# Four blocks in one transfer, or two and two: splitting an early load of a conditional residual kernel

## The reference

```python
# L0: a weight per sample, folded from 8 masked weights
w_bot = einsum('bg,got->bot', y, weight * mask)
x = x + einsum('bnt,bot->bno', x, w_bot) + bias
# L1: base linear layer and 8 LoRA pairs of rank 16, weighted by cond_8, scaled by 2
h = einsum('btc,erc->bter', x, As)
x = x + x @ W_base.T + b_base + 2 * einsum('bter,eor,be->bto', h, Bs, w)
# L2: top 2 of 8 experts (gelu(gate) * up, hidden 512) and one shared expert of the same form
# L3: one expert of 8 by argmax (silu(up) * gate, hidden 256, with biases)
```

## Time and profile before

| what | value |
|---|---|
| median of 3 runs | 137.72 us (137.63 to 138.63) |
| profiled execution | 138.17 us |
| its span, first to last instruction | 136.3 us |
| TensorE busy | 131.7 us |
| VectorE, ScalarE, GpSimd busy | 102.0, 99.4, 75.4 us |
| granted TensorE clock | 1.00 throughout |

### The profile page before, as it was taken

How to read it: one execution, slowest core, us unless ns; L and a number is a source line. 1 busy time by engine, 2 the same in 40 slices (tenths; PEclk the granted TensorE clock), 3 DMA queues, 4 the chain that set the end, 5 groups by cost and what they waited for, 6 DMA issues and landing times.

```text
span 136.3 us, 3164 instructions
## 1 busy us (share of the span) xinstructions
PE 131.7 (97%) x866; PEld 119.4 (88%) x866; DVE 102.0 (75%) x201; ACT 99.4 (73%) x205; POOL 75.4 (55%) x89
## 2 busy tenths in 40 slices
PE   7899999999999999999999999999999999999990
PEld 5778888888888879999999999999999999999990
DVE  0599898797757666668877687767878677887892
ACT  3774797979964659777797777756757669889870
POOL 0148369776991045468496684963452635325770
PEclk9999999999999999999999999999999999999999
DMA  4999999997002974674764657646577474755134
GB/s 141 356 404 407 408 400 402 396 402 301 7 0 93 373 302 190 279 281 197 300 267 197 257 224 293 282 184 267 225 282 297 172 287 195 290 239 227 45 112 154
DMA packets 11489, 34.54 MB, mean 253 GB/s; under 512 B 1104, under 2 KB 2512, under 8 KB 11472
## 3 DMA queue, kind: packets, MB, share of 16 engines
q1 hardware_dynamic: 11184, 34.15, 63.8%
q10 hardware_dynamic: 288, 0.20, 0.5%
HBM read 12.32 MB, written 1.05 MB: 98 GB/s over the span
## 4 chain that ended last, share of the span: by engine, by line
PE 75%; DMA 7%; POOL 7%; DVE 3%; SPq 3%; issue 2%; ACT 2%; DVEq 0%; POOLq 0%; ACTq 0%
PE up L297 26%; PE gate L297 26%; PE acc L297 23%; POOL slabs L765 7%; DMA w_gu<-slabs 4%; DMA slabs<-third_in 3%; SPq L223 1%; DVE up L930 1%; SPq L280 1%; ACT slabs L640 1%; DVE x_res L910 1%; DVE x_res L939 1%; ACT h_pair L635 0%; DVE x_lo L902 0%; ACT x_hi L612 0%
## 5 line engine op out<-in xcount | busy, mean ns | idle before, releaser
L772 POOL TENSOR_TENSOR dn_lo<-slabs,dn_hi 128x256 fp32r<-128x256 f32 x40 | 29.6, 741 | 40.5 <-ACT dn_hi L653 40.5
L629 ACT ACTIVATE h_act<-gate 128x512 f32<-128x512 f32 x48 | 28.8, 601 | 26.2 <-PE gate L297 24.9
L922 DVE TENSOR_TENSOR h_pair<-up,h_pair 128x512 fp32r<-128x512 f32 x55 | 37.6, 683 | 0.0
L932 DVE SCALAR_TENSOR_TENSOR up<-h_act,w_route,up 128x512 f32<-128x512 f32 x32 | 24.2, 756 | 17.0 <-PE up L297 16.6
L297 PE MATMUL gate<-x_hi,w_gu 128*128 128x256 f32 x160 | 35.2, 282 | 0.2 <-DMA w_gu<-slabs 0.2
L297 PE MATMUL up<-x_hi,w_gu 128*128 128x256 f32 x158 | 34.5, 281 | 0.0
L635 ACT ACTIVATE h_pair<-up 128x512 fp32r<-128x512 f32 x55 | 32.8, 597 | 0.0
L297 PEld LDWEIGHTS gate<-x_hi,w_gu 128*128 128x128 f32 x160 | 27.3, 188 | 1.0 <-issue 0.9
L297 PE MATMUL acc<-h_pair,dn_hi 128*128 128x512 f32 (+1 forms) x76 | 27.5, 377 | 0.0
L297 PEld LDWEIGHTS up<-x_hi,w_gu 128*128 128x128 f32 x158 | 27.0, 188 | 0.0
L297 PE MATMUL gate<-x_lo,w_gu 128*128 128x256 f32 x80 | 22.4, 280 | 0.0
(11 more groups left out here) (128 smaller groups left out, 203.0 us busy)
## 6 DMA issues: line engine op xcount, KB each, us to landing
w_gu<-slabs SPq DMA_DIRECT2D x40, 512.0 KB, 3.0
slabs<-slabs_moe SPq DMA_DIRECT2D x8, 768.0 KB, 13.5
slabs<-slabs_l SPq DMA_DIRECT2D x4, 768.0 KB, 8.7
sh_raw<-slabs_shared SPq DMA_DIRECT2D x2, 384.0 KB, 5.3
x_res<-x_rest SPq DMA_DIRECT2D x1, 768.0 KB, 7.0
outT<-x_res SPq DMA_DIRECT2D x6, 128.0 KB, 1.9
slabs<-second_in SPq DMA_DIRECT2D x1, 320.0 KB, 3.1
slabs<-third_in SPq DMA_DIRECT2D x1, 256.0 KB, 4.2
```

Source lines behind the costliest of these rows:

```text
L629: nc.scalar.activation(h_act[:, u % 2, :], gate_ps[u % 2][:], ACT.Gelu_apprx_tanh).then_inc(act_done, 1)
L772: nc.gpsimd.tensor_tensor(dn_lo[:, q % W_SLOTS, :], slab_cols(at, DOWN_AT, 256), dn_hi[:, q % W_SLOTS, :].bitcast(F32), ALU.subtract).then ...
L922: V.tensor_tensor(h_lo[:, u % H_SLOTS, :], h_of(u), h_hi[:, u % H_SLOTS, :].bitcast(F32), ALU.subtract).then_inc(h_lo_done, 1)
L932: ins = V.scalar_tensor_tensor(h_of(u), h_act[:, k, :], weight, h_of(u), ALU.mult, ALU.mult)
```

## The change

third_in is cut in two. Blocks 6 and 7 stay in it, 128 KB. The mask and the LoRA down matrix become a transfer mask_in of their own, 128 KB too, with a semaphore d_mask. It is issued on SP right behind the third, ahead of the fourth. DVE waits for d_mask where it waited for d_third; TensorE still waits for d_third before block 6, and has a new wait for d_mask before lora(0,2). Addresses in the on-chip memory stay as they were, since the two buffers lie side by side.

```diff
-        third_sb = early(4, P)
+        third_sb = early(2, P)
+        mask_sb = early(2, P)
-        lora_bT, mask, lora_a = second_sb[:, 4, :], third_sb[:, 2, :], third_sb[:, 3, :]
+        lora_bT, mask, lora_a = second_sb[:, 4, :], mask_sb[:, 0, :], mask_sb[:, 1, :]
...
             sp.dma_start(third_sb[:, :, :], third_in).then_inc(d_third, DMA)
+            sp.dma_start(mask_sb[:, :, :], mask_in).then_inc(d_mask, DMA)
             sp.dma_start(fourth_sb[:, :, :], fourth_in).then_inc(d_fourth, DMA)
...
+            pe.wait_ge(d_mask, DMA)
             pe.wait_ge(bw_ready, 1)
             lora(gate_ps[0][:, 0:S], 0, 2)
...
-            dve.wait_ge(d_third, DMA)
+            dve.wait_ge(d_mask, DMA)
...
-    third = cat([w_l0[:, 6:], a(L0_cond_mask)[:, None], as_[:, None]], axis=1)
+    mask_in = np.stack([a(L0_cond_mask), as_], axis=1)
...
-        "second_in": second, "third_in": third, "fourth_in": fourth,
+        "second_in": second, "third_in": w_l0[:, 6:], "mask_in": mask_in, "fourth_in": fourth,
```

More of the change, by code:

```diff
@@ L67, with build @@
 C_COLS = C_W + 2 * P
-def build(nc, x_first, first_in, second_in, third_in, fourth_in, x_rest, slabs_moe, slabs_l3, slabs_shared, outT):
+def build(nc, x_first, first_in, second_in, third_in, mask_in, fourth_in, x_rest, slabs_moe, slabs_l3, slabs_shared, outT):
     with ExitStack() as ctx:
@@ L169, in build @@
         m_banks = [None, gate_ps[1][:, 0:S], up_ps[1][:, 0:S], acc_ps[:, S:2 * S]]
-        d_first, d_second, d_third, d_fourth, d_x, d_x_rest = (
-            sem(n) for n in ("d_first", "d_second", "d_third", "d_fourth", "d_x", "d_x_rest"))
+        d_first, d_second, d_third, d_mask, d_fourth, d_x, d_x_rest = (
+            sem(n) for n in ("d_first", "d_second", "d_third", "d_mask", "d_fourth", "d_x", "d_x_rest"))
         d_expert = [sem(f"d_expert{e}") for e in range(E)]
```

## The result

| what | before | after |
|---|---|---|
| median of 22 runs each | 137.90 us | 138.54 us |
| ratio after / before | | 1.0048, 95% interval 1.0027 to 1.0069 |
| profiled execution, its span | 138.17, 136.3 us | 138.54, 136.7 us |

The ratio and its interval rest on the fast runs alone; of the changed kernel's 22, three stand outside (139.64, 140.68, and 218.46 us at a granted clock of 0.567), and the median of the other 19 is 138.45.

What follows compares the result with a forecast made beforehand. The front bounds the kernel: from the third transfer through mask and DVE to TensorE's almost unbroken work. Terms 0 + 0.1 + 0 + 0 + 0 gave +0.1 us on the 137.72 median: 137.8 us, range 137.0 to 138.7.

Steps and rivals of the forecast that it cites:

- the sum: Whole kernel: the terms 0 + 0.1 + 0 + 0 + 0 add up to +0.1 us.
- (1): Third transfer, cut to 128 KB: lands 0.35 us earlier, at 5.5, with TensorE's fold matmuls at 5.55 to 6.26.
- (2): TensorE's earlier front: at most 0.1 to 0.2 us remain, ending at matrix(1), which waits for DVE; worth 0.
- (3): Landing of mask and LoRA down matrix: 0.1 us later than 5.85, with ends of -0.7 and +0.7.
- (4): DVE's chain from the mask on: shifts +0.1 us; a hit of 0.49 us might gain up to 0.26, taken as 0.
- Rival B: Mask's own transfer lands late, at DVE's first masking and TensorE's lora(0,2): 0.7 us slower, 138.4 us; chance 0.2.
- (5): SP's issues after the third, 0.47 us later: only 0.1 us remains, hidden by slack, first shared slab included; worth 0.
- The signs that were named: Changed profile: third lands 0.3 to 0.4 us earlier, L848 at 5.9 to 6.1, no DVE gap, gate at 11.2 to 11.3.
- three signs of being wrong: L848 over 0.3 us from 5.94, a DVE gap before 10 us, or the gate's start moving without the end following.
- rival E: Mask's transfer pays its own fixed part: lands 2.35 us later, at 8.2, DVE's chain with it, 140.1 us; chance 0.02.

Runs made afterwards that it cites:

- e1: The changed kernel timed again with no edit; ratio 1.0041 against the kernel before.
- f3: The changed kernel with GpSimd's split of the first shared slab in two halves, TensorE's first unit waiting only for its half; ratio 1.0046 against the kernel before.
- e3: Blocks 6 and 7 alone in the third transfer, mask and LoRA down matrix in the fourth, as many transfers as before; ratio 1.0019 against the kernel before.
- e4: The changed kernel with the first shared slab issued ahead of x_first; ratio 1.0003 against the kernel before.
- e2: The changed kernel with its two transfers read out of one main-memory tensor; ratio 1.0049 against the kernel before.
- e6: The changed kernel with the mask's transfer issued by ScalarE instead of SP; ratio 1.0007 against the kernel before.
- e8: The kernel before timed again with no edit; ratio 0.9996.
- e5: The kernel before with one more transfer of 8 KB, read by nobody, behind the third; ratio 1.0058.
- e7: The kernel before with the first shared slab issued ahead of x_first; ratio 0.9979.
- f1: The kernel before with one extra 8 KB transfer issued behind the second shared slab; ratio 1.0012.
- f2: The kernel before with two extra small transfers behind the third; ratio 1.0075.
- f4: The kernel before with the first shared slab ahead of x_first and GpSimd's split of it in two halves; ratio 0.9995.

## Why the prediction held, and what it missed

The time lies in the range because the range was wide: it held the scatter of three runs and 0.7 us to either side. By the sum the change would have cost 0.1 us; that 0.66 still fell inside is luck, not the mechanism.

**The start, (1).** "Landing at 5.5" was beaten in the first profile, 4.73, and in e1, 4.63 (1.63 + 3.0). But with 128 KB it also landed at 5.43 (f3), 5.73 (e3) and 5.93 (e4). Over seven profiles each the mean is 5.19 with 128 KB (also e2 and e6, both 4.93) and 5.40 with 256 KB (5.85, e8 5.63, e5 5.03, e7 5.23, f1 5.13, f2 5.23, f4 5.73). So the cut brings some 0.2 us, less than the 0.35 of the sum, and the late landing of before comes back now and then.

**No value at the end, (2).** Right in its result: matrix(1) waited for DVE as before, 0.24 us against 0.34. But TensorE's fold matmuls did not go at 5.55 to 6.26; they ended at 6.80 (6.84 in e1), since they were slower themselves (last section), and in the first profile DVE waited for them. e3, with the mask later and the blocks not, agrees that DVE's chain is the longer path there, within what one profile can say.

**The mask, (3) and (4).** Forecast +0.1 with ends of -0.7 and +0.7. Masking began at 5.64, 6.02, 5.86 (e2), 5.92 (f3) and 6.39 (e4) in the five profiles with this order, against 5.94, 5.68 (e8), 5.81 (e7), 5.56 (f1) and 5.85 (f4) in the five with the old order up to the fourth transfer. The mean is 5.97 against 5.77: 0.2 later, and the profiles scatter by 0.4 and 0.75. That fits the 0.1, and can't tell it from 0.3. The hit that (4) took at 0.49 took 0.23 in the first profile, as GpSimd's add had moved off it; DVE then waited for TensorE for as long. Rival B had the right sign and nearly the right size, 0.7 us, but named the wrong transfer.

**The later issues, (5).** This is the step that failed. It said of the first shared slab: "0.17 to spare", "What remains is the same 0.1", "Worth 0". The 0.17 was right for ScalarE. But the step named as the slab's reader the gate at 11.16, which reads the high part, and left out the low part, which GpSimd makes (9.29 to 11.12) and TensorE loads at 11.48. And the delay was not 0.1: measured over profiles with the slab behind x_first, it lands at 7.97 on average without a further transfer ahead of it on SP's queue (before, e8, f1, e6, e3), and at 9.23 with one (after, e1, e2, f3, e5): 1.26 us later. Of this 0.47 is the later issue. The argument that waiting in line swallows an issue's delay would have needed the queue to go on at its rate, and it did not: 233 to 335 GB/s in the seven profiles with one or two more transfers ahead of the fourth on SP's queue, 354 to 398 in the seven others. (From 2.50 to 8.50 the same two groups read 289 to 341 and 343 to 372, so they part, but e5 and e3 lie side by side.) A landing at 8.15 + 0.47 = 8.62 would still have been covered; 9.23 is 0.61 us past it. This is about what the ratio shows (0.66), and what TensorE's first sh_lo product shows: 12.52, 12.38 and 11.81 after, e1 and e2 (mean 12.24), against 11.71 and 11.36 in the two profiles of before (mean 11.54), 0.70 later. That the three agree so well is partly chance: in e5, with the same loss, the product started at 11.32, and in e3, e4, e6 and e7, without a loss, at 12.06 to 12.25.

The point of method in it: the slack was read from one row (slab lands 8.15, ScalarE starts 8.32) and the price of the delay was set at 0.1, with no range. With the 0.47 of the issue as the other end, the 0.17 would have been overrun by 0.3 us, and the chain behind it (ScalarE, GpSimd's 1.8 us, TensorE at 11.48) would have been written down as a rival.

**The signs that were named.** The gate came at 11.2 to 11.3 and matrix(1) waited for DVE, as said. L848 started at 5.64, outside 5.9 to 6.1 and just at the limit of 0.3 us from 5.94; DVE had gaps before 10 us; and the gate moved by 0.1 while the end moved by 0.4. By two of its three signs of being wrong the prediction was wrong, and by the third at the limit. e1 meets the first two (6.02, no gap) and misses the third.

**Fixed part, rival E.** Fell, as forecast: the mask landed 0.57 us after the blocks (4.73, and 2.10 + 3.2 = 5.30). The Trainium skill (DMA: Bandwidth & Descriptors, Bandwidth) advises to batch. The sign of that advice holds at this place, as e5 shows with 8 KB for 0.8 us, and not at the later one of f1. Its fixed part of 2.0 us, which the page fits for transfers issued by GpSimd and not by SP, was not paid.

**Open.** Why one more transfer in this place lowers the rate of those behind it, for 3 us or more, isn't shown. e2 speaks against the tensor, e5 against the bytes and the cut rows, f1 against an extra transfer as such; e6 suggests that the same transfers in another queue do less harm. The packets of the traces say where the rate goes, not why: of those over 512 bytes that start from 5.50 to 8.50, the median takes 121 ns in all fourteen profiles, but 10 to 20 take over 400 ns in the seven profiles with the lower rate, and 1 to 9 in the others. Open too is how much of the 0.66 us goes by the mask (0.2 us by the means above) and how much by the slab.

## What to carry to other kernels

A transfer that is put into a queue shifts each one behind it, so before a split at the front, list every later transfer of the queue with its landing, its first reader, and the slack of the whole chain behind that reader; the one with the least slack sets the price, and it need not be near the edit. Here it was the first slab, 0.47 us of cover and three engines deep, while the path that the split shortened had none of the end's time in it. Follow every reader: the first one may read what is ready, and the second what an engine between them still has to make. Where an early transfer must be cut, issue the new piece from another queue (1.0007 against 1.0048) or move the transfer with the thinnest cover forward (1.0003); here neither was faster than not cutting. And a cover given to the first reader only may hand its wait to the next.

## What the runs showed of the hardware

How long TensorE's fold matmuls take differs from execution to execution, though TensorE works from 0.76 us on, with the same first row of 2.90 us, in all. Groups of TensorE's fold matmuls from 4.5 to 6.0 us, kernel before and kernel after (count, busy us, mean ns):

```profile
L297 PE MATMUL up<-cond_all,slabs 128*128 128x128 f32 x9 | 1.5, 298 | 0.4 <-DMA slabs<-third_in 0.4
```

```profile
L299 PE MATMUL up<-cond_all,slabs 128*128 128x128 f32 x8 | 1.9, 421 | 0.0
```

The timeline of the kernel after shows twelve such records in one run, up to 6.8 us, where the eight of before took 1.16:

```profile
4.30 1.16 PE L297 MATMUL up<-cond_all,slabs 128*128 128x128 f32 x8
```

```profile
4.43 2.37 PE L299 MATMUL up<-cond_all,slabs 128*128 128x128 f32 x12
```

The granted clock reads 1.00, its upper level (2.4 GHz), in the windows of both, so the column names no cause; that the slower matmuls ran at the lower level (1.2 GHz) would be a guess from their length, 421 ns against 298, and no row shows it. It isn't the change: in the kernels with the old order up to the third transfer the twelve take from 1.76 us (f1) to 2.57 (f2), and in those with the change's from 1.59 (e2) to 2.64 (e4). Where the fold ends late DVE's first masking may wait for TensorE instead of for a transfer (0.92 us in the rows above), and an earlier landing of the blocks is worth nothing even on TensorE's own path. It moves the front by more than the change does: where the fold ended at 7.06 or later (e4, e6, e7, f2) the gate started at 11.52 to 11.70, and in the nine profiles with an end at 6.84 or earlier and the mask not put back to the fourth transfer, at 10.77 to 11.29.

The other surprise is the rate of the queue told above: with 8 KB more in front of it (e5), the 3 us from 5.50 on move 307 GB/s in place of 389.
